# Attention with masked keys in the softmax: the masked keys' share of three chunks' row sums, moved from whole rows on GpSimd to the 16-column layout of the reciprocals

## The reference

```python
xn = layernorm(x)
q, k, v = xn @ Wq, xn @ Wk, xn @ Wv          # 16 heads of 32
scores = (q . k) * tril(ones)                # a masked score is 0, not minus infinity
attn = softmax(scores / T ** 0.5)            # T = 2048; masked keys take part with exp(0 - max)
s = (attn @ v) @ Wo
g = silu(layernorm_affine(xn) @ ternary(weight).T + bias)
out = x + s * g
```

## Time and profile before

| | |
|---|---|
| median of 3 runs | 1534.5 us (1533.64 to 1537.15) |
| the profiled execution | 1533.04 us, span 1531.3 us |
| mean granted clock of PE | 0.993 of full speed |
| PE busy | 1484.9 us, 97% of the span |
| DVE, ACT, POOL busy | 68%, 51%, 57% |
| DMA | 201 MB, 131 GB/s on average |

### The profile page before, as it was taken

The page is one execution under the profiler, slowest core; times in us unless marked ns, Lnnn a source line. Parts: engine busy times, 40 slices in busy tenths (PEclk is TensorE's granted clock), DMA queues, the critical chain, the costliest instruction groups (busy, mean ns, idle before and its releaser), DMA issues. The chain is left out here.

```text
span 1531.3 us, 24566 instructions
## 1 busy us (share of the span) xinstructions
PE 1484.9 (97%) x8554; PEld 899.1 (59%) x8554; DVE 1045.5 (68%) x2413; ACT 773.8 (51%) x1614; POOL 865.7 (57%) x723
## 2 busy tenths in 40 slices
PE   5999999999999999999999999999999999999898
PEld 4788888888544455555554545545455554543586
DVE  7546666544787777777777777777777777773367
ACT  4333322332545656656566566656666666667211
POOL 4100000000566878778887787877878778777501
PEclk9999999999899999999999999999999999999999
DMA  6568965548824514242450542424155161124588
GB/s 208 180 183 233 262 188 164 165 142 216 227 49 113 123 39 104 85 105 53 116 118 23 140 110 50 106 86 105 42 124 113 30 139 51 51 83 138 187 300 307
DMA packets 118348, 201.26 MB, mean 131 GB/s; under 512 B 23216, under 2 KB 40752, under 8 KB 117200
## 3 DMA queue, kind: packets, MB, share of 16 engines
q1 hardware_dynamic: 118224, 199.69, 47.5%
HBM read 123.02 MB, written 76.09 MB: 130 GB/s over the span
## 5 line engine op out<-in xcount | busy, mean ns | idle before, releaser
L885 POOL TENSOR_TENSOR acc<-acc,Pb 128x1024 f32<-128x1024 f32 (+2 forms) x308 | 598.9, 1974 | 150.8 <-PE psO L1444 128.0
L1015 ACT ACTIVATE Pb<-psS 128x512 f32<-128x512 f32 (+2 forms) x1122 | 518.4, 532 | 302.0 <-PE psS L1421 291.7
L1132 DVE TENSOR_REDUCE mx<-psM 128x1 f32<-128x512 f32 x768 | 484.5, 683 | 148.8 <-PE psM L1321 147.6
L1421 PE MATMUL psS<-half 97*128 97x512 f32 (+1 forms) x1247 | 475.0, 398 | 12.3 <-ACT Pb L1015 8.9
L1321 PE MATMUL psM<-half 96*128 96x512 f32 (+3 forms) x1280 | 457.6, 383 | 8.0 <-DVE mx L1129 3.1
L1421 PEld LDWEIGHTS psS<-half 97*128 97x128 f32 x1247 | 234.3, 190 | 252.3 <-issue 104.9
L1321 PEld LDWEIGHTS psM<-half 96*128 96x128 f32 x1280 | 235.3, 190 | 79.3 <-DVE mx L1132 28.7
L1129 DVE CUSTOM_DVE_ANT_0 psM<-psM,negm 128x256 f32<-128x256 f32 (+3 forms) x512 | 238.3, 518 | 56.7 <-PE psM L1321 56.1
L1444 PE MATMUL psO<-Pb,Vs 128*32 128x512 f32 (+3 forms) x2304 | 266.9, 534 | 2.2 <-POOL Pb L868 2.2
L1149 DVE TENSOR_TENSOR st_lo<-psP,st_hi 128x512 fp32r<-128x512 f32 x64 | 43.9, 688 | 118.7 <-ACT st_hi L977 118.7
L1450 PE MATMUL psL<-Pb,ones 128*32 128x512 f32 (+3 forms) x1072 | 124.8, 535 | 0.0
(11 more groups left out here) (103 smaller groups left out, 1478.2 us busy)
## 6 DMA issues: line engine op xcount, KB each, us to landing
half<-q_hi SPq DMA_DIRECT2D x32, 512.0 KB, 9.8
half<-k_hi SPq DMA_DIRECT2D x32, 512.0 KB, 9.7
xt<-in_L_attn_x SPq DMA_DIRECT2D x8, 1024.0 KB, 8.2
q_hi<-st_hi SPq DMA_DIRECT2D x32, 256.0 KB, 4.5
q_lo<-st_lo SPq DMA_DIRECT2D x32, 256.0 KB, 4.8
gate<-gs SPq DMA_DIRECT2D x32, 256.0 KB, 2.2
k_hi<-st_hi SPq DMA_DIRECT2D x32, 256.0 KB, 2.8
k_lo<-st_lo SPq DMA_DIRECT2D x32, 256.0 KB, 2.9
```

The source lines that it names most:

```text
L885: g.tensor_tensor(to[:, :, o:], to[:, :, o:], Pb[s % RING][:, heads, o:], ALU.add).then_inc(sum_done, 1)
L1015: a.activation(weights(s, h)[:, o:], score_bank(s * HQ + h, last)[:, o:], ACT.Exp, scale=SCALE).then_inc(exp_done, 1)
L1132: ins = v.tensor_reduce(flat[:, heads, slots], bank[:, 0:ns * w].rearrange("p (a b c) -> p a b c", a=nh, c=w), AX.X, ALU.max)
L1421: t.matmul(score_bank(n, last)[:, o:], Ks[par][j // HALF][0:MROW + 1, h, j % HALF * P:(j % HALF + 1) * P], Qs[par][c // 2][0:MROW + 1, h, ...
```

## The change

For chunks 0 to 2, POOL's iota and the product later * E are gone, and DVE's addition of E to psL becomes a copy. In their place: SP loads the negative maxima a second time in the 128 x 16 layout (ec), ACT takes their exponential, POOL multiplies them with counts made once at the start, and POOL adds the product to lc after lc's transfer. The reciprocal on DVE waits for that addition. The counts are an iota on POOL and four operations on DVE at the start of the kernel. Chunk 3 stays as it was.

```diff
+COUNTED_AT = {FIRST[1] + 1: 0, FIRST[2] + 3: 1, FIRST[3] + 1: 2}
...
+        counts = sbuf(top, "counts", [P, NDIV, HQ * CW // P], F32)
...
+        ec = [sbuf(pc, f"ec{i}", [P, HQ * CW // P], F32) for i in range(2)]
...
@@ SP, load_chunk
+                if c < NDIV:
+                    sp.dma_start(ec[i][:], m_rows[bass.ds((NCH * m + c) * HQ, HQ), :].rearrange("h (a w) -> (h a) w", w=HQ * CW // P)).then_inc(ec_in[i], 16)
...
@@ POOL, start
+            g.iota(counts[:], pattern=[[-CW, NDIV], [-1, HQ * CW // P]], base=T - 1, channel_multiplier=-(HQ * CW // P),
+                   allow_small_or_imprecise_dtypes=True).then_inc(counts_made, 1)
...
@@ POOL, quad
                 def later_keys(qn, c):
                     i, k = c % 2, qn * NCH + c
-                    pool.wait_ge(NE_done, START + k).then_inc(pool_waited, 1)
-                    g.iota(later[:], pattern=[[-1, CW]], base=T - 1 - c * CW, channel_multiplier=0,
-                           allow_small_or_imprecise_dtypes=True).then_inc(later_done, 1)
                     pool.wait_ge(sub_done, START + k + 1)
                     pool.wait_ge(E_done, START + k + 1)
                     g.tensor_tensor(cum[i][:], cum[i][:], E[i][:], ALU.mult).then_inc(SE_done, 1)
-                    pool.wait_ge(SE_done, START + k + 1)
-                    pool.wait_ge(later_done, START + k + 1)
-                    g.tensor_tensor(E[i][:], later[:], E[i][:], ALU.mult).then_inc(NE_done, 1)
+                    if c == NCH - 1:
...
+                def add_counts(qn, c):
+                    i = c % 2
+                    pool.wait_ge(ec_done, qn * NDIV + c + 1)
+                    pool.wait_ge(counts_done, HQ)
+                    g.tensor_tensor(ec[i][:], ec[i][:], counts[:, c, :], ALU.mult).then_inc(ecm_done, 1)
+                    pool.wait_ge(lc_in, (qn * NDIV + c + 1) * HQ * 16)
+                    pool.wait_ge(ecm_done, qn * NDIV + c + 1)
+                    g.tensor_tensor(lc[:], lc[:], ec[i][:], ALU.add).then_inc(lcs_done, 1)
...
+                    if gr in COUNTED_AT:
+                        add_counts(qn, COUNTED_AT[gr])
                     if gr in DIVIDED_AT:
                         divide(qn, DIVIDED_AT[gr])
...
@@ ACT, quad
+            def exp_counted(qn, c):
+                i = c % 2
+                act.wait_ge(ec_in[i], (qn * (2 - i) + c // 2 + 1) * 16)
+                a.activation(ec[i][:], ec[i][:], ACT.Exp, scale=SCALE).then_inc(ec_done, 1)
...
                 for gr, (c, j) in enumerate(GROUPS):
+                    if gr in COUNTED_AT:
+                        exp_counted(qn, COUNTED_AT[gr])
                     exps(qn, 2 * gr + 1, not more)
...
@@ DVE, start
+            dve.wait_ge(counts_made, 1)
+            for h in range(HQ):
+                rows = counts[h * DH:(h + 1) * DH]
+                v.tensor_scalar(rows, rows, float(h * CW), None, ALU.add).then_inc(counts_done, 1)
             dve.wait_ge(w_in[0], 16)
...
@@ DVE, denominators
                 dve.wait_ge(L_full, START + k + 1)
-                dve.wait_ge(NE_done, START + k + 1)
-                v.tensor_tensor(E[i][:], psL[:], E[i][:], ALU.add).then_inc(lst_done, 1)
+                if c < NDIV:
...
+                    dve.wait_ge(SE_done, START + k + 1)
+                    v.tensor_copy(E[i][:], psL[:]).then_inc(lst_done, 1)
+                else:
+                    dve.wait_ge(NE_done, START + qn + 1)
+                    v.tensor_tensor(E[i][:], psL[:], E[i][:], ALU.add).then_inc(lst_done, 1)
...
@@ DVE, quad
                         if s in RECIPROCALS_AT:
-                            dve.wait_ge(lc_in, (qn * NDIV + RECIPROCALS_AT[s] + 1) * HQ * 16)
+                            dve.wait_ge(lcs_done, qn * NDIV + RECIPROCALS_AT[s] + 1)
                             v.reciprocal(lc[:], lc[:]).then_inc(lc_done, 1)
```

More of the change, by code:

```diff
@@ L438, in build @@
         later_done = sem("later_done")
+        counts_made = sem("counts_made")
+        counts_done = sem("counts_done")
+        ec_in = [sem(f"ec_in{i}") for i in range(2)]
+        ec_done = sem("ec_done")
+        ecm_done = sem("ecm_done")
+        lcs_done = sem("lcs_done")
         sum_done = sem("sum_done")
@@ L507, in attention_over @@
             eng.wait_ge(L_full, START + NQUAD * NCH)
-            eng.wait_ge(NE_done, START + NQUAD * NCH)
+            eng.wait_ge(NE_done, START + NQUAD)
             eng.wait_ge(ost_done, START + NQUAD * NCH)
@@ L894, in later_keys @@
                     g.tensor_tensor(cum[i][:], cum[i][:], E[i][:], ALU.mult).then_inc(SE_done, 1)
-                    pool.wait_ge(SE_done, START + k + 1)
-                    pool.wait_ge(later_done, START + k + 1)
-                    g.tensor_tensor(E[i][:], later[:], E[i][:], ALU.mult).then_inc(NE_done, 1)
+                    if c == NCH - 1:
+                        pool.wait_ge(NE_done, START + qn).then_inc(pool_waited, 1)
+                        g.iota(later[:], pattern=[[-1, CW]], base=T - 1 - c * CW, channel_multiplier=0,
+                               allow_small_or_imprecise_dtypes=True).then_inc(later_done, 1)
+                        pool.wait_ge(SE_done, START + k + 1)
+                        pool.wait_ge(later_done, START + qn + 1)
+                        g.tensor_tensor(E[i][:], later[:], E[i][:], ALU.mult).then_inc(NE_done, 1)
+                def add_counts(qn, c):
[6 more added lines that the diff above has]
+                    g.tensor_tensor(lc[:], lc[:], ec[i][:], ALU.add).then_inc(lcs_done, 1)
                 def divide(qn, c):
```

## The result

The kernel after took 1599.33 us (median of 4 runs, 1594.18 to 1601.26) against 1535.83 for the kernel before beside it: a ratio of 1.0409 (95% interval 1.0381 to 1.0438), 63.5 us more. The direction was as forecast; the size was nearly four times the forecast's 16.5 us and outside its range. The profiled execution had a span of 1597.8 us at a mean granted clock of 0.968, against 1531.3 at 0.993.

The account below looks back on a forecast made before the run. TensorE, busy 97% of the span, bounds the kernel; 12.9 (chunk 2) + 3.0 (chunk 0) + 1.0 (division) + 0.6 (start) - 1.0 (POOL's relief) = +16.5 us on 1534.5, giving 1551.0, range 1540 to 1558 us.

Parts of the forecast that it names:

- The reasoning on PE's banks: Three banks only DVE empties: PE's fourth maxima matmul, needing the first's bank, begins 0.85 us after the reciprocal.
- chunk 2: Reciprocal waits behind POOL's additions; PE's fourth maxima matmul 2.07 us late in quads 0 to 6, 12.9 us net.
- Pair of operations: POOL's two added 128x16 operations per chunk: 0.21 us each plus 0.08 hand-over, 0.50 us; ends 0.25 and 2.1.
- The rival of dear small operations: POOL's small operations take 1.0 us each, 1.6 us more in 15 places: +24, 1575 in all; 5%.
- chunk 0: Reciprocal waits for POOL's pair; PE's fourth maxima matmul 0.43 us late in quads 1 to 7, 3.0 us.
- The copy out of psL: DVE's copy replacing its sum of psL and E takes 0.68 us, as long as the sum; no gain.
- the rival of a held copy: DVE's copy stands until POOL's running addition ends, 1.2 us on average, 24 times: +17, 1568 in all; 4%.
- the division: POOL's division in quad 7 comes 1.0 us later because d_rows goes out later; PE waits for selects: +1.0 us.
- PE's first product: At the start DVE writes counts ahead of x's low parts, holding up this product: 4 x 0.15 = 0.6 us.
- POOL's relief: 42 us off POOL brings selects before diagonals sooner; 1 us gained, ends 0 and 9.9; as rival 1526, 4%.
- Chunk 1 ... nothing: POOL's pair done by 605.7, DVE's reciprocal comes at 612.58, so no loss in chunk 1.
- the busy time of PE hardly changes: Sign in the profile after: POOL's busy time falls by about 30 us while TensorE's stays nearly the same.

Follow-up runs that it names:

- neither_wait: Kernel after, POOL's addition to lc replaced by a second product with counts, without POOL's wait for lc's transfer or DVE's for POOL: 1533.88 us, ratio 0.9981.
- dve_waits_only: Kernel after, POOL's addition to lc replaced by a product that waits for no transfer; DVE's reciprocal still waits for POOL: 1572.00 us, ratio 1.0227.
- dose4: Kernel before with four idle DVE reductions of 512 columns behind the reciprocal of chunk 2, nothing of the change: 1574.05 us, ratio 1.0256.
- pool_waits_only: Kernel after, POOL's addition to lc replaced by a product that still waits for lc's transfer; DVE's reciprocal doesn't wait for POOL: 1559.27 us, ratio 1.0144.
- lc_first: Kernel after with only chunk 1's lc transfer moved ahead of the half loads in SyncE's queue: 1579.97 us, ratio 1.0283.
- dose2: Kernel before with two idle DVE reductions of 512 columns behind the reciprocal of chunk 2, nothing of the change: 1547.01 us, ratio 1.0076.

## Why the prediction was right and wrong

**Right: what bounds, and the direction.** The wait of DVE for POOL, with the row maxima behind it, is one of two that take the place of the work removed. The reasoning on PE's banks held to hundredths: 0.85 us from the reciprocal to PE's fourth matmul.

**Right: chunk 2.** 7 x 2.07 us forecast, seven waits of 2.00 to 2.02 measured. Pair of operations: 0.50 us taken, 0.58 measured from the first one's start at 643.40 to 643.98; each operation 0.21 taken, 0.22 measured. The rival of dear small operations was out.

**Right: chunk 0.** 0.43 us a quad forecast, 0.21 to 0.39 measured, 2.4 us in seven quads against 3.0.

**Right, small terms.** The copy out of psL is 0.68 us, as taken, in all 24 cases (678 to 692 ns): the rival of a held copy was out. In quad 7 the division follows the one before it by 14.46 us (1460.72 to 1475.18) and not by 13.24, 1.2 us where 1.0 was taken. PE's first product waits 1.8 us and not 1.46: 0.3 where 0.6 was taken. POOL's relief less the start's cost comes to 2.4 us by neither_wait, where I had 0.4; the place is not the one I named (see below).

**Wrong: "Chunk 1 ... nothing".** I read only when DVE's reciprocal came (612.58) and found the pair done well ahead. The pair's second operation has a wait of its own, for lc's transfer; I had named it in the part on POOL and never asked when that transfer lands in chunk 1. The front of the text had the answer to hand: in SyncE's queue divisors 1 stands behind the half loads. By the reciprocal's row the transfer of chunk 1 was in no hurry, since DVE met it later; POOL meets it some 7 us sooner (605.7 by my working), with a diagonal's selects behind. In the kernel before the four pieces were issued from 596.50 on and took 14.0 us to land, so it was not there before 610.5. Measured: 51.7 us of waits of POOL, 12.7 us of waits of PE, and 23 us in time.

**Wrong: "the busy time of PE hardly changes".** The sum took a wait of PE to cost its length. Of the forecast's own term, the waits of chunks 0 and 2, 15 us of waiting cost 35.8 us by dve_waits_only and, without anything of the change, 38.6 by dose4. This is the greater error: PE's busy time rose by 41.7 us. The Trainium skill, TensorE: Matmul & The Clock Gate, describes a kin of it in the section "A second HAM failure mode: psum-queue depth-cycling": brief and frequent idle times between groups of matmuls, where banks are passed around, bring the clock down again and again. The prediction did not weigh it. These traces agree that idle times at the banks bring the clock down, but here single waits do it in a stream that is otherwise full: 0.50 behind waits of 2.0 us, and 1.00 behind those of 0.86 us. The trace of before had a case of its own: in its table by stretch the clock is down to 0.60 in quad 7, behind a wait of PE of 3.21 us for ACT (until 1424.41) and around one of 2.21 us for POOL (until 1428.80),

```profile
1424.00:1432.00 8.00, 5.32 (x22) 2.84 (x26) 0.00 (x0) 3.39 (x12) 8.00 (x11) 0.60 0.04 15
```

and I had read no clock there, only that of a steady quad.

**How it adds up.** In waits of PE: 15.1 us for row maxima (forecast 15.9) and 12.7 for chunk 1; in halved clock 41.7 by PE's busy time; together 69.5 of the span's 66.5. What was given back is in one row, PE's waits for ACT's exponentials: 5.5 us in 6 places where the kernel before has 8.9 in 11. neither_wait shows the same; the row in the kernel before and in neither_wait:

```profile
PE psS L1421 <- ACT Pb L1015: 8.9, 11, 3.2
```
```profile
PE psS L1468 <- ACT Pb L1045: 4.8, 5, 3.2
```

Gone in it are six waits of 0.60 to 0.92 us, one each in quads 1 to 6 (577.71 in quad 1), in the first steps of chunk 1 behind the selects of chunk 0's diagonal, 4.1 us in all. My term counted only PE's waits for the selects themselves.

The range could not hold the loss, since both of its ends were built from waits alone.

**Open.** pool_waits_only has 12.2 us more busy time for 12.6 us of waits, dve_waits_only 25.8 for 15.2: waits of like length cost the clock differently, and the runs don't say why. In part it is the execution: pool_waits_only's profiled one has a clock of 0.987, its other three 0.982 to 0.983. Beyond that, length alone doesn't decide. The clock stayed at 1.00 behind a wait of 1.82 us in quad 4 of the kernel after, 1.76 us in quad 6 of pool_waits_only, and 2.00 us in quad 0 of lc_first, PE's timeline and the ten us around:

```profile
508.06 0.49 PE L1367 MATMUL psM<-half 96*128 96x512 f32 x1 [2.00 <-DVE mx L1173]
```
```profile
506.00:516.00 10.00, 8.00 (x48) 4.14 (x47) 7.29 (x29) 4.59 (x10) 7.13 (x7) 1.00 0.27 81
```

Nor was it tried which part of POOL's relief takes away the six waits for ACT.

## What to carry to other kernels

When an operation moves to another engine, list each wait that goes with it, and look up for each, in each place where it occurs, when what it waits for arrives, not just when its result is needed. Cost a wait of the bounding TensorE by its length only while it is short; where a forecast has waits of some 2 us, look in the trace for the granted clock behind waits as long. A small operation in an in-order queue is dear by what stands behind it: the repair was to move it past the work that others wait for, by one step on DVE and two groups on POOL, and not to hurry its input.

## What was unexpected of the hardware

- **The clock.** PE's granted clock went from 1.00 to about 0.5 (1.2 in place of 2.4 GHz) at single waits in a stream of matmuls that was otherwise full, for about 3 to 10 us. Of the waits of 2.0 us at step (3, 3) all seven did it in the kernel after and in dve_waits_only, six of seven in lc_first. Of those between 1.3 and 1.9 us some did (1.61 and 1.43 us) and some did not (1.72, 1.44 and 1.82 us); of those of 0.83 to 0.87 us in dose2 none did. Seven waits of about 2 us cost as much again in clock and more.
- **DVE beside POOL.** An operation of 128x16 with two inputs in SBUF took 5.1 us in the median beside POOL's additions, 0.17 at the least; one with one input in the same place 0.25. In 13 of 24 cases it waited until POOL's run of three or more instructions had ended.
- **Small transfers.** lc's four pieces of one row each landed after 1.7 us in the median and some 14 us when issued right behind six half loads.
